# Rows of the last eight groups of each gather fetched one by one from SyncE and ScalarE

## What is computed

```
x = x + relu(segment_sum((N0 @ W0[r])[src, type] * weight, dst))
Z = segment_sum(relu(concat(N1[src], edge64) @ M.T + mb), dst)
x = x + relu(concat(N1, Z) @ U.T + ub)
x = x + segment_sum((N2 @ W2[r])[src, type], dst)
x = x + layernorm(mlp((1+eps)*N3 + segment_sum(N3[dst] + edge16 @ We + be, src)))
```

## Time and profile before

| | us |
|---|---|
| median of 3 runs | 26913.0 |
| span of the profiled execution, first to last instruction | 22991.7 |
| what lies around the span (difference to the median) | 3921.3 |
| busy in the span: TensorE, VectorE, ScalarE, GpSimd | 9432.7, 10159.5, 1783.1, 15546.8 |
| gather stages "g0", "g1", "g2", about | 4060, 4130, 4040 |

### The profile page before, as it was taken

The page is one execution under the profiler, slowest core; times in us unless marked ns, Lnnn a source line. Parts: engine busy times, 40 slices in busy tenths (PEclk is TensorE's granted clock), DMA queues, the critical chain, the costliest instruction groups (busy, mean ns, idle before and its releaser), DMA issues. The chain is left out here.

```text
span 22991.7 us, 207917 instructions
## 1 busy us (share of the span) xinstructions
PE 9432.7 (41%) x48147; PEld 7206.5 (31%) x48150; DVE 10159.5 (44%) x25131; ACT 1783.1 (8%) x4849; POOL 15546.8 (68%) x16453
## 2 busy tenths in 40 slices
PE   2777776433333333333333633333332222222366
PEld 1333333233333333333333333333331111111254
DVE  7777777544444443333333432222224333333473
ACT  4000000000000000000000200000001111111100
POOL 2777777777777757777777267777776777777400
PEclk7555555555555555555555655555555555555686
DMA  3333332222222222222222322222223222222462
GB/s 103 99 98 98 99 98 77 69 64 61 61 64 61 64 40 66 61 61 61 61 61 61 83 78 64 61 64 61 61 61 66 83 82 83 83 82 82 133 221 70
DMA packets 1005113, 1785.47 MB, mean 78 GB/s; under 512 B 352294, under 2 KB 461123, under 8 KB 1004534
## 3 DMA queue, kind: packets, MB, share of 16 engines
q1 hardware_dynamic: 484294, 1127.71, 15.7%
q0 software_dynamic: 513696, 654.80, 12.5%
q10 hardware_dynamic: 7056, 2.21, 0.0%
HBM read 1279.37 MB, written 510.79 MB: 78 GB/s over the span
## 5 line engine op out<-in xcount | busy, mean ns | idle before, releaser
L1031 PE MATMUL psum<-arena 128*128 128x64 f32 x19392 | 4447.7, 424 | 7932.5 <-DMA arena<-table,arena 4593.2
L932 POOL DMA_INDIRECT arena<-table,arena x6464 | 6108.0, 945 | 2006.7 <-issue 1927.4
L1031 PEld LDWEIGHTS psum<-arena 128*128 128x128 f32 x19392 | 4227.4, 330 | 8153.0 <-issue 6213.6
L983 DVE TENSOR_TENSOR arena<-arena,psum 128x64 f32 x9696 | 2150.8, 222 | 6335.1 <-PE psum L1031 4421.4
L700 POOL DMA_INDIRECT rec<-arena x3125 | 3003.1, 961 | 1376.6 <-issue 948.7
L1136 POOL DMA_INDIRECT rec<-arena x3232 | 3180.9, 984 | 1093.7 <-issue 970.4
L932 POOL DMA_INDIRECT arena<-ptable,arena x3232 | 3148.0, 974 | 998.1 <-issue 984.7
L477 PE MATMUL psum<-arena 128*128 128x196 bf16 (+1 forms) x4375 | 1378.8, 429 | 1265.0 <-DVE arena L608 1264.9
L1155 DVE TENSOR_TENSOR arena<-psum,arena 128x1024 bf16<-128x1024 f32 x404 | 494.6, 1224 | 2715.2 <-DMA arena<-rec 2715.2
L1203 PE MATMUL psum<-arena 128*128 128x128 bf16 x3232 | 418.2, 311 | 2527.4 <-DVE arena L1155 2527.4
L1203 PEld LDWEIGHTS psum<-arena 128*128 128x128 bf16 x3232 | 312.9, 141 | 2674.0 <-DVE arena L1155 2346.4
(11 more groups left out here) (194 smaller groups left out, 10126.3 us busy)
## 6 DMA issues: line engine op xcount, KB each, us to landing
arena<-rec SPq DMA_DIRECT2D x303, 1408.0 KB
arena<-rec SPq DMA_DIRECT2D x440, 488.0 KB, 4.4
arena<-in_edge SPq DMA_DIRECT2D x625, 232.0 KB, 2.6
arena<-rec SPq DMA_DIRECT2D x404, 352.0 KB, 3.3
arena<-table,arena POOLq DMA_INDIRECT x6464, 2.4
rec<-arena POOLq DMA_INDIRECT x6357, 2.3
table<-arena SPq DMA_DIRECT2D x196, 512.0 KB
arena<-ptable,arena POOLq DMA_INDIRECT x3232, 2.4
```

The costliest lines, as they stand in the source:

```text
L932: nc.gpsimd.indirect_dma_start(rows[q][:, j * D:(j + 1) * D], None, tab, bass.IndirectOffsetOnAxis(ap=idx[:, j, field:field + 1], axis=0)) ...
L983: v.tensor_tensor(block_sum, block_sum, ps[q % SB][:, j * D:(j + 1) * D], ALU.add).then_inc(s_add[j], 1)
L1031: last = nc.tensor.matmul(ps[q % SB][:, j * D:(j + 1) * D], hot[q % SB][:, j * P:(j + 1) * P], rows[q][:, j * D:(j + 1) * D], start=True, ...
```

## The change

Of the 404 groups, GpSimd's gather and all that hangs on it now cover `NEAR = 396`: 32 turns and a rest of 12 groups. The last `HG = 8` groups ("far" groups) are fetched otherwise. Each of their 1024 rows has a DMA of its own, of 256 bytes to one partition, with the table row in a register. SyncE issues those of partitions 0 to 63, ScalarE those of 64 to 127. One far group is fetched in the time of `BATCH = 4` turns. For it each of the two engines loads 512 row numbers with a strided DMA into one partition (`take_indices`) and waits for them, then loads eight of them at a time into registers and issues eight DMAs (`fetch_rows`). SyncE puts up to 6 such steps behind each load of records (11 slots of the 12 in a batch have some: ten times 6 and once 4). In "g1" ScalarE puts one or two such steps behind each relu, 64 over 48 groups. At the end of a batch both wait until their rows have landed (`all_landed`). After the four turns VectorE and TensorE "visit" the far group: one-hot, in "g1" the sum and a relu of ScalarE, 8 matmuls into a bank of their own, 8 adds. SyncE also loads the lanes, weights and `R_Q` words of all far groups once, within turn 0 (`far_fields`): 16 DMAs in "g0" and "g1", 8 in "g2". The new buffers lie in the space of `hparts` (`shared`), which is free during a gather.

```diff
@@ -62,6 +62,10 @@
 SB = 4
 RS = 8
 AHEAD = 2
+HG = 8
+BATCH = 4
+NEAR = GROUPS - HG
+assert HG * BATCH <= (NEAR - 1) // RG and NEAR % RG % LG == 0
 KEYS = 2
...
     rows = [b.take(G * D) for _ in range(RG)]
     hot = [b.take(G * P) for _ in range(SB)]
-    assert b.at <= ARENA - NB * D
+    farhot = b.take(G * P)
+    fard, farw = b.take(HG * G), b.take(HG * G)
+    extra = Buffers(shared)
+    far, farq, picks = extra.take(HG * G * D), extra.take(HG * G * D), extra.take(P * G, I32)
+    assert b.at <= ARENA - NB * D and extra.at <= NB * PARTS * D // 2
+    ENDS = HG * (1 + weighted + relu_q)
...
+    psf = psum[:, 3584:4096]
+    TURNS = (NEAR - 1) // RG
+    REST = NEAR - TURNS * RG
+    HALF = P // 2
+    fars = rec[NEAR * G * P:GROUPS * G * P, :].rearrange("(g p j) w -> p g j w", p=P, j=G)
+    fars = [fars[:, h] for h in range(HG)]
+    far_rows = rec[NEAR * G * P:GROUPS * G * P, field:field + 1].bitcast(I32)
+    def take_indices(engine, semaphore, h, half):
+        at = half * (HALF * G)
+        with nc.allow_non_contiguous_dma("one word of a record"):
+            engine.dma_start(picks[0:1, at:at + HALF * G].rearrange("o (r w) -> o r w", w=1),
+                             far_rows[bass.ds(h * (P * G) + at, HALF * G), :].rearrange("(o r) w -> o r w", o=1)).then_inc(semaphore, 16)
+        engine.wait_ge(semaphore, h * 16 + 16)
+        engine.sem_inc(s_taken)
+    def fetch_rows(engine, regs, h, part):
+        half = part // HALF
+        engine.load(regs, picks[0:1, part * G:(part + 1) * G])
+        for j in range(G):
+            row = engine.snap(regs[j], min_val=0, max_val=tab.shape[0] - 1)
+            engine.dma_start(far[part:part + 1, bass.ds(h * (G * D) + j * D, D)], tab[bass.ds(row, 1), :]).then_inc(s_far[half][j % 4], 16)
+    def all_landed(engine, h, half):
+        for n in range(4):
+            engine.wait_ge(s_far[half][n], h * (HALF * G // 4 * 16) + HALF * G // 4 * 16)
+        engine.sem_inc(s_landed[half])
+    def in_batches(engine, step, visit):
+        step(0)
+        with engine.Fori(1, BATCH) as i:
+            step(i)
+        visit(0)
+        with engine.Fori(1, HG) as h:
+            with engine.Fori(h * BATCH, h * BATCH + BATCH) as i:
+                step(i)
+            visit(h)
+        if HG * BATCH < TURNS:
+            with engine.Fori(HG * BATCH, TURNS) as i:
+                step(i)
...
         @block.sync
         def _(sp):
-            def step(i, groups=RG):
-                for k in range(groups // LG):
-                    for q in range(k * LG, (k + 1) * LG):
-
-                        wait_earlier(sp, s_g[q], i * (16 * G))
-                    wait_earlier(sp, s_sum[q] if relu_q else s_hot[q], i)
-                    sp.dma_start(loads[k].rearrange("p (g w) -> p g w", g=LG), recg[:, bass.ds(i * RG + k * LG, LG), :]).then_inc(s_ld[k], 16)
-            peeled(sp, TURNS, step)
-            step(TURNS, REST)
+            regs = [sp.alloc_register(f"{name}_row{j}") for j in range(G)]
+            def load(i, k):
+                for q in range(k * LG, (k + 1) * LG):
+                    wait_earlier(sp, s_g[q], i * (16 * G))
+                wait_earlier(sp, s_sum[q] if relu_q else s_hot[q], i)
+                sp.dma_start(loads[k].rearrange("p (g w) -> p g w", g=LG), recg[:, bass.ds(i * RG + k * LG, LG), :]).then_inc(s_ld[k], 16)
+            def far_fields():
+                for h in range(HG):
+                    mine = slice(h * G, (h + 1) * G)
+                    with nc.allow_non_contiguous_dma("one word of a record"):
+                        sp.dma_start(fard[:, mine].rearrange("p (j w) -> p j w", w=1), fars[h][:, :, R_DSTL:R_DSTL + 1]).then_inc(s_ends, 16)
+                        if weighted:
+                            sp.dma_start(farw[:, mine].rearrange("p (j w) -> p j w", w=1), fars[h][:, :, R_W:R_W + 1]).then_inc(s_ends, 16)
+                    if relu_q:
+                        sp.dma_start(farq[:, h * G * D:(h + 1) * G * D].rearrange("p (j f) -> p j f", f=D),
+                                     fars[h][:, :, R_Q:RW]).then_inc(s_ends, 16)
+            def batch(h):
+                parts = -(-HALF // (BATCH * (RG // LG)))
+                for t in range(BATCH):
+                    for k in range(RG // LG):
+                        load(h * BATCH + t, k)
+                        at = (t * (RG // LG) + k) * parts
+                        if at == 0:
+                            take_indices(sp, s_pick, h, 0)
+                        for part in range(at, min(at + parts, HALF)):
+                            fetch_rows(sp, regs, h, part)
+                    if isinstance(h, int) and t == 0:
+                        far_fields()
+                all_landed(sp, h, 0)
+            peeled(sp, HG, batch)
+            if HG * BATCH < TURNS:
+                with sp.Fori(HG * BATCH, TURNS) as i:
+                    for k in range(RG // LG):
+                        load(i, k)
+            for k in range(REST // LG):
+                load(TURNS, k)
...
-            def step(i, groups=RG):
+            def step(i, groups=RG, more=True):
                 for q in range(groups):
-                    if groups == RG or q + AHEAD < groups:
+                    if more or q + AHEAD < groups:
...
+            def visit(h):
+                dve.wait_ge(s_ends, 16 * ENDS)
+                lanes = fard[:, bass.ds(h * G, G)].rearrange("p (j o) -> p j o", o=1).to_broadcast([P, G, P])
+                ones = farhot.rearrange("p (j w) -> p j w", w=P)
+                wait_earlier(dve, s_fmm, h)
+                if weighted:
+                    v.tensor_tensor(ones, iotas, lanes, ALU.is_equal).then_inc(s_fis, 1)
+                    dve.wait_ge(s_fis, h + 1)
+                    v.tensor_tensor(ones, ones, farw[:, bass.ds(h * G, G)].rearrange("p (j o) -> p j o", o=1).to_broadcast([P, G, P]),
+                                    ALU.mult).then_inc(s_fhot, 1)
+                else:
+                    v.tensor_tensor(ones, iotas, lanes, ALU.is_equal).then_inc(s_fhot, 1)
+                if relu_q:
+                    for half in range(2):
+                        dve.wait_ge(s_landed[half], h + 1)
+                    mine = far[:, bass.ds(h * (G * D), G * D)]
+                    v.tensor_tensor(mine, mine, farq[:, bass.ds(h * (G * D), G * D)], ALU.add).then_inc(s_fsum, 1)
+                dve.load(regs, blkd[0:1, bass.ds(h * G + NEAR * G, G)])
+                ats = [dve.snap(reg, min_val=0, max_val=(NB - 1) * D) for reg in regs]
+                dve.wait_ge(s_fmm, h + 1)
+                wait_earlier(dve, s_add[G - 1], h * (BATCH * RG) + (BATCH * RG - 1))
+                for j in range(G):
+                    block_sum = acc[:, bass.ds(ats[j], D)]
+                    v.tensor_tensor(block_sum, block_sum, psf[:, j * D:(j + 1) * D], ALU.add).then_inc(s_fadd, 1)
+                    dve.wait_ge(s_fadd, h * G + (j + 1))
             for q in range(AHEAD):
                 one_hots(0, q)
-            peeled(dve, TURNS, step)
-            step(TURNS, REST)
+            in_batches(dve, step, visit)
+            step(TURNS, REST, False)
             add_group(TURNS, REST - 1)
         @block.scalar
         def _(act):
+            regs = [act.alloc_register(f"{name}_rowa{j}") for j in range(G)]
+            def relu(i, q):
+                act.wait_ge(s_sum[q], i + 1)
+                nc.scalar.activation(rows[q], rows[q], ACT.Relu).then_inc(s_msg, 1)
+            def batch(h):
+                take_indices(act, s_picka, h, 1)
+                if not relu_q:
+                    for part in range(HALF, P):
+                        fetch_rows(act, regs, h, part)
+                else:
+                    turns = BATCH * RG
+                    for n in range(turns):
+                        relu(h * BATCH + n // RG, n % RG)
+                        for part in range(HALF + HALF * n // turns, HALF + HALF * (n + 1) // turns):
+                            fetch_rows(act, regs, h, part)
+                all_landed(act, h, 1)
+                if relu_q:
+                    act.wait_ge(s_fsum, h + 1)
+                    mine = far[:, bass.ds(h * (G * D), G * D)]
+                    nc.scalar.activation(mine, mine, ACT.Relu).then_inc(s_fmsg, 1)
+            peeled(act, HG, batch)
             if relu_q:
-                def step(i, groups=RG):
-                    for q in range(groups):
-                        act.wait_ge(s_sum[q], i + 1)
-                        nc.scalar.activation(rows[q], rows[q], ACT.Relu).then_inc(s_msg, 1)
-                peeled(act, TURNS, step)
-                step(TURNS, REST)
+                if HG * BATCH < TURNS:
+                    with act.Fori(HG * BATCH, TURNS) as i:
+                        for q in range(RG):
+                            relu(i, q)
+                for q in range(REST):
+                    relu(TURNS, q)
...
+            def visit(h):
+                pe.wait_ge(s_fhot, h + 1)
+                if relu_q:
```

(10 more changed lines are left out.)

18 lines of the change are left out of this document (10 added, 8 removed).

## The result

The kernel after took 34767.99 us (median of 4 runs, 34762.19 to 34792.35) against 26917.02 us before (4 runs, 26902.59 to 26931.47): a ratio of 1.2922 [1.2904, 1.2941], 7851 us slower. The forecast was 26754, and 27370 the end of its range.

A forecast was written before the change was run, and what follows sets the result against it. The prediction took the number of GpSimd's DMAs to bound each gather. Removing DMAs gives -241.8 us, the first batches lose 82.5, so -159: 26913 becomes 26754 us, range 26680 to 27370.

The forecast's parts named there:

- The 3921 us around the span I hold constant: Whole kernel: the 3921 us of timed median beyond the profile's span was taken as unchanged by the change.
- the rest: Outcomes outside the forecast and the three rivals, mostly the time around the span; chance 0.03.
- The bound: All three gathers: the number of GpSimd's DMAs sets the pace, about 1.25 to 1.28 us each; other engines follow.
- the ceiling of 241.8 us: All three gathers: the most the change can bring, from 64 fewer GpSimd DMAs in each.
- The price of a step: SyncE and ScalarE: p, one load of eight registers plus eight row DMAs, takes 6.8 us, bounds 6.0 to 8.1.
- the DMA instruction: Each row on SyncE and ScalarE: 0.317 us, the mean of 0.303 and 0.332, within 0.58 a row.
- rival 1: SyncE's steps are short, p up to 6.3, so only indices and `far_fields` are lost: -195, 26718 us; chance 0.15.
- The fixed part of a batch: SyncE: 15 us beside 64 steps: 12 loads at 0.7, an index load at about 3.5, the landing at 3.
- The rule: Against the change: 512 sequencer cycles, 0.43 us, for a copy instruction would make a step some 0.9 us longer.
- The first batch: Start of each gather: SyncE's steps delay record loads, so GpSimd loses 32.6, 23.3 and 26.6 us, sum 82.5.
- Rival 2: SyncE's record loads and ScalarE's "g1" relus wait behind steps, becoming the bound: +449, 27362 us at p = 7.6; chance 0.31.
- Rival 3: Gathers: row DMAs slow GpSimd's own by 0.029 us each, 276 in all: +117, 27030 us; chance 0.06.

The follow-up runs named there:

- b0_again: The kernel before, unchanged, profiled again: 27030.59 us, ratio 1.0001, span 27019.4 us.
- e15: The kernel after with each row's destination fixed, independent of the batch counter, so a row is one piece; free: 22681.69 us, ratio 0.9861.
- e11: The kernel after with each engine's 512 row DMAs of a batch replaced by one block DMA; free: 22668.15 us, ratio 0.9872.
- e1: The kernel after with each engine's 512 row DMAs of a batch replaced by one block DMA; held up: 27069.45 us, ratio 1.0026.
- a1: The kernel after, unchanged, run again where the engines run freely: 23712.34 us, ratio 1.0324.
- e7: The kernel before with 8000 one-row DMAs to fixed places on idle ScalarE in each of "g0" and "g2"; held up: 29254.24 us, ratio 1.0811.
- e2: The kernel after with SyncE's 512 row DMAs of a batch replaced by one block DMA, ScalarE's rows kept; held up: 32794.92 us.
- e5: The kernel after with four far groups instead of eight, each over eight turns instead of four; held up: 29064.13 us.
- e8: The kernel after with one indirect DMA of GpSimd for each near group in place of eight; free: 23447.94 us, ratio 1.0216.
- e6: The kernel before with 400 turns of an empty loop on idle ScalarE in each of "g0" and "g2"; held up: 27052.03 us, ratio 1.0002.

## Why the prediction was wrong

**Two prices, told apart by one table** (us, median; difference to the kernel before of the same set; the first column's "after" is the result's):

| | held up | free |
|---|---|---|
| kernel before | 26917 to 27050 | 22953 to 22999 |
| after | 34768 (+7851) | 23712 (+747) |
| rows of one piece | 32147 (+5096) | 22682 (-318) |
| without the rows | 27069 (+51) | 22668 (-298) |

**"The 3921 us around the span I hold constant": this step failed first and cost most.** They lay in the stages, as hold-ups of every engine but GpSimd, and the change puts 24576 row DMAs, each with register instructions around it, on such engines with other work queued behind. The front named the difference of span and median, and a span is the time of its execution but for 2 us, in after and in b0_again alike. A median 17% over the span of the same kernel meant that the profile was of another kind of execution. I took no rival from it and gave it 3 in 100 with "the rest".

**The bound**: right in the free kind (the ceiling of 241.8 us came out as 243.7 in e15 and 257 in e11), wrong in the timed one, where e1 gains nothing. VectorE's 1939.5 us of waiting were slack in the free execution only.

**The price of a step**: 6.8 us, bounds 6.0 to 8.1; measured 7.97. The register load was sized too high (2.0 with its gaps; 1.67 without) and the row too low: 0.776 us from start to start against 0.58. The term that failed is the DMA instruction. I took the mean of 0.303 and 0.332; it was 0.228 to 0.238 with a constant target and 0.547 with one that holds the batch counter. Line 447's 0.355 had its register on the DRAM side, so none of my rows had one on the SBUF side, and it costs pieces, not arithmetic. I named the second register address as what spoke against rival 1, and priced only its arithmetic. The fixed part of a batch was 15 us, measured 27: the loop's jump back and a landing of indices that took twice the 3.5.

**The rule** of the Trainium skill, "DMA: Bandwidth & Descriptors" ("Why a DMA increments its semaphore by 16 and not by 1"), would give an estimate of 0.43 us for a copy instruction. The trace shows 0.23 for one piece and 0.55 for sixteen, so neither is the figure of the Trainium skill. The advice of the Trainium skill on the same page ("Rules for kernel authors"), to coalesce small transfers, stood against the change, and after was slower in both kinds; with one piece a row the same 24576 small transfers were faster in the free kind (-318 us).

**The first batch**: forecast to lose 82.5 us in all. With a step of 5.5 us it fits: in a1 batch 0 of "g0" takes 412.5 us, less than GpSimd's 480, with one piece a row and the slots as they were. So the piece alone decides whether a batch fits. It is the later batches that don't, the other way round. In e15 GpSimd waits for records 33.5 us in "g0", 16.8 more than in the earlier trace rows.

**Rival 2** is what happened in the free kind. It was put at p = 7.26 and up for SyncE, with 27362 (+449) at 7.6 and over +1000 at 8.1; measured +747 at 7.97. The mechanism, the place (record loads behind the steps) and the order of size hold. The relus behind ScalarE's steps in "g1", its second place, don't show in the free kind: "g1" lost less (+201) than "g0" and "g2", and all three last 4329 to 4333 us, SyncE's batches.

**Rival 3**, row DMAs slowing GpSimd: out in the free kind, where line 1019's DMAs take 0.944 us in a1 and 0.945 in the earlier trace rows, with the same 0.30 us between them. Held up, e7's gathers are at most 73 us longer.

**What makes the held-up loss ten times the free one** is a circle, read from after and e2 to e5, not tried by itself. While GpSimd gathers a slot, 40 us, SyncE is held up and issues 12 of its 48 rows (in "g0" of after, 3.8 us a row). Then GpSimd runs out of records and stops, and only in that stop of 42 us SyncE does the other 36 and the next load: 66 to 82 us a slot where a1 has 48.7 and e15 40. The end of a hold-up at a stop of GpSimd, in "g0" of after:

```profile
9102.27 0.95 POOL L1019 DMA_INDIRECT arena<-table,arena  x1 [0.30 <-issue]
...
9108.75 0.22 DVE L1070 TENSOR_TENSOR arena<-arena,psum 128x64 f32 x1 [1.17 <-issue]
9109.53 0.27 PE L1167 MATMUL psum<-arena 128*128 128x64 f32 x1 [2.64 <-issue]
...
9111.77 2.64 PE L1167 MATMUL psum<-arena 128*128 128x64 f32 x12 [1.98 <-issue]
```

GpSimd's last DMA is over at 9103.2; until 9111 instructions trickle, then twelve matmuls come in 2.64 us.

**What stays open**: why one execution is held up and another isn't (chip, neighbours or hour), and whether it is GpSimd's indirect DMAs that hold the others up or something that coincides with them, for e8 never met a held-up execution. One rival wasn't tried at all: that the recording of the instructions takes part. In after 1043 of 27163 direct DMA instructions have a recorded duration below 0.1 us, in a1, the same kernel running freely, none (line 943's least is 229 ns), so the recorded times themselves are disturbed; and no run here is known to have been timed without such records. Open is also whether a version of the change exists that gains where the engines are held up. e1, without any row DMA, says no for this structure.

## What to carry to other kernels

Compare the profile's span with the timed median before anything else. Here they agreed within 2 us in every execution that has both; where they differed by 3921, the profile was of another kind of execution than the timed ones, and every slack in it was suspect; a change that adds instructions to engines which look idle is the one it misleads about most.

Before many small DMAs are put on a queue, look at the address form of both ends. A register in the SBUF address of a row cut it into 16 pieces and made the instruction 547 ns instead of 228; a fixed buffer, with steps that start two slots later, turned +747 us into -318. Look also at what stands behind such rows: SyncE's alone, ahead of the record loads, gave 7179 of the 7749 us held up, and ScalarE's alone, with only the visit behind them, 5776.

## What the runs showed of the hardware that I had not expected

- In held-up executions the engines other than GpSimd start an instruction only every 0.7 to 1.4 us each, or none at all for up to 36 us ("g1" of b0_again). It sets in some 15 to 20 us after GpSimd starts to issue indirect DMAs back to back, and in the stretch above it outlasts GpSimd's stop by some 8 us. Register instructions and branches of ScalarE are drawn out too (35 and 45 ns in the median, up to 1408 in e6). GpSimd's own DMAs keep 0.947 us. The kernel before took some 4000 us longer with it.
- The jump back to the top of a long unrolled loop took SyncE 5.6 us (5868.9 to 5874.5 in a1), once in a batch.
- Between each gather and the next stage some 20 us were gained by the change in the free kind (17 to 24 in e15, e11 and a1); why wasn't tried.
